# Attention half of a fused layer on eight cores: gram products reordered, three operations moved on ACT and DVE

## The chip, the cores and the metric

The kernel runs on all 8 NeuronCores of one Trainium2 chip, each with two of the sixteen sequences. A core has five engines that run their own instruction lists and meet by semaphores: TensorE (PE in the rows; its weight loads are PEld), VectorE (DVE), ScalarE (ACT), GpSimd (POOL) and SyncE (SP, here only DMA). The time is the device time in microseconds of the slowest core.

## What is computed

A pre-norm layer: x + attention(layernorm(x)), then x + ffn(layernorm(x)). The change touches the attention part only. Its core, per chunk of 64 rows and for 16 heads of 64:

```python
k = k / norm(k)
scores = q @ k.T * scale                 # 64 x 64 per head and chunk, masked
chunk_out = softmax(scores) @ v + 0.1 * (q @ M)
# then 64 sequential steps on the state M of 64 x 64:
M = M - alpha * (M k_t) k_t^T + beta * v_t k_t^T
```

The kernel does not take the 64 steps one by one. With G = k k^T (the gram matrix) the steps are a triangular system, solved by a product of six factors (I + A)(I + A^2)(I + A^4)... with A from -alpha G.

## The kernel before

phase_a (the attention half) works on NT = 32 tiles of 128 rows, a tile holding one chunk of 64 rows of each of the core's two sequences, 16 heads x 64 = 1024 columns. phase_b (the choice of experts and the two layers of the ffn) starts when phase_a has ended, and is not changed.

phase_a is one software-pipelined loop over i = -1 .. NT + 2, written out by hand for each engine, in the functions pe, act, dve, pool and sync. In iteration i the engines work on several tiles at once: i + 2 is normalised (stats, ln_steps, normal), i + 1 is transposed (x_turn), tile i is projected to k, v and q (proj), tile i - 1 = j gets its gram matrix and scores, tile i - 2 = u is solved (solve), and tile i - 3 = e ends: last factors, state update, output projection (ends). Each engine takes its instructions strictly in the order written, so an instruction that waits on a semaphore holds all that stand behind it.

PSUM: psD0 and psD1 (projections, transposes), psW (factors), and psXY, whose halves are psX (powers of A) and psY (row sums, state, outputs). gram_and_scores(j) fills both halves of psXY: 32 products, for each head h and sequence s one of a 64x64 weight (k_fm) with 128 columns (kaq_fm, holding -alpha k and q side by side). Head h writes columns hrow(h) * 128, and hrow(h) = (h % 2) * 8 + h // 2, so the even heads land in psX and the odd ones in psY. The product's place in the 128x128 array is (r, s * 64) with r = (h % 2) * 64: even heads use rows 0 to 63, odd ones rows 64 to 127, and s picks the column half.

The steps that matter, by name and line:

- TensorE, in the order of its loop: state_h(e) (L642) writes psY; state_m(e) (L653) waits for s_h; k_by_h(u) (L668) waits for s_h and s_m; q_part (L540); power_b(u, 3) (L597); factor(u, 0) (L630); row_sums(u) (L677); k_turn(i) (L551); gram_and_scores (L586), which waits for s_ka, s_qfm, s_b and s_lden; factor(u, 1); wo_part(e, 0) (L569), which waits for s_kfm; power_a(u, 4) (L597), which waits for s_g and s_exp of tile j.
- ACT: B's copy (L415), ln_steps (L405 and L407: logarithm and exponential on 128x1), rden's logarithm of the row sums in psY (L475) and its exponential (L477), then the copy of g (L483) and the exponential of the scores, PT (L484), which both read psXY.
- DVE: at an iteration's start AI[5], and the copies W, W and Wf (L829), then plus_eye 0 and 1 (AI = A + I, L825), the addition to H_sb (L868), the row sum of k's squares (L871) and its maximum with a constant (L873), plus_eye 2, the addition to M_sb (L880), xnf (L883), RHS (L886), stats (L808 to L811), plus_eye 3, W (L829), xn_tm (normal, L817), k_fm (L898), W.

Of the kernel before, what the change touches and what calls it, by code (L numbers as in the profile page):

```python
# [15 lines left out]
NH = 16  # L16
NT = 32
# [20 lines left out]
def hrow(h):  # L38
    return (h % 2) * 8 + h // 2
# [84 lines left out]
def choice_ln(s, env, n):  # L124
    rstd, s_ln = env["rstd_y"][n % 2], env["s_yln"]
    s.wait_ge(env["s_ystat"], 3 * n + 3)
    if n > 1:
        s.wait_ge(env["s_y"], n - 1)
    s.activation(rstd[:, 0:1], env["mv_y"][n % 2][:, 1:2], AF.Ln, bias=env["cst"][:, 0:1]).then_inc(s_ln, 1)  # L129
    s.wait_ge(s_ln, 2 * n + 1)  # L130
    s.activation(rstd[:, 1:2], rstd[:, 0:1], AF.Exp, scale=-0.5).then_inc(s_ln, 1)
# [9 lines left out]
def phase_a(nc, ctx, sb, ps, sem, env):  # L141
# [64 lines left out]
    s_lden = sem("s_lden")  # L206
# [8 lines left out]
    with ExitStack() as pa:  # L215
# [55 lines left out]
        def heads(ap):  # L271
            return ap.rearrange("p (h c) -> p h c", c=64)

        def by_mask(m):
            return m[:, :].unsqueeze(1).broadcast_to([128, 16, 64])
# [5 lines left out]
        def xbuf(t):  # L281

            return x_sb[(t + 3) % 7]
# [118 lines left out]
        def act(s):  # L402
            def ln_steps(t):
                s.wait_ge(s_stat, 3 * t + 3)
                s.activation(rstd[:, 0:1], mv[:, 1:2], AF.Ln, bias=cst[:, 0:1]).then_inc(s_ln, 1)  # L405
                s.wait_ge(s_ln, 2 * t + 1)
                s.activation(rstd[:, 1:2], rstd[:, 0:1], AF.Exp, scale=-0.5).then_inc(s_ln, 1)  # L407

            def power_a(u, k):
                s.wait_ge(s_pa, 5 * u + k)  # L410
                s.copy(A[k][:], psX).then_inc(s_a, 1)  # L411

            def power_b(u, k):
                s.wait_ge(s_pb, 4 * u + k)
                s.copy(B[k][:], psX).then_inc(s_b, 1)  # L415

            def k_half(i, hf):
                s.wait_ge(s_pk, 2 * i + hf + 1)
                s.copy(kraw[:, hf * 512:hf * 512 + 512], (psD0, psD1)[hf][:, :]).then_inc(s_kraw, 1)  # L419

            def v_half(i, hf):
                s.wait_ge(s_pv, 2 * i + hf + 1)
                s.copy(v_tm[i % 3][:, hf * 512:hf * 512 + 512], (psD0, psD1)[hf][:, :]).then_inc(s_v, 1)

            def q_half(i, hf):
                s.wait_ge(s_pq, 2 * i + hf + 1)
                if i > 0:
                    s.wait_ge(s_tq, i)
                s.copy(q_tm[:, hf * 512:hf * 512 + 512], (psD0, psD1)[hf][:, :]).then_inc(s_q, 1)  # L429

            s.wait_ge(s_prep, 2)
            ln_steps(0)
            def o_copy(e):
                s.wait_ge(s_po, e + 1)
                s.copy(o_fm[:, :].rearrange("p (a s c) -> p s a c", a=8, s=2),  # L435
                       psY.rearrange("p (s a c) -> p s a c", s=2, a=8)).then_inc(s_o, 1)

            for i in range(-1, NT + 3):
                u, e, j = i - 2, i - 3, i - 1
                proj = 0 <= i < NT  # L440
                solve = 0 <= u < NT
                if 0 <= e < NT:
                    o_copy(e)
                if proj:
                    k_half(i, 0)
                if solve:
                    power_a(u, 1)
                if proj:
                    k_half(i, 1)
                if solve:  # L450
                    power_b(u, 1)
                if proj:
                    v_half(i, 0)
                if solve:
                    power_a(u, 2)
                    power_b(u, 2)
                if proj:
                    s.wait_ge(s_kmax, i + 1)
                    s.activation(rk[:], kss[:], AF.Ln).then_inc(s_rk, 1)
                    s.wait_ge(s_rk, 2 * i + 1)  # L460
                    s.activation(rk[:], rk[:], AF.Exp, scale=-0.5).then_inc(s_rk, 1)  # L461
                    v_half(i, 1)
                if solve:
                    power_a(u, 3)
                if proj:
                    q_half(i, 0)
                if solve:
                    power_b(u, 3)
                if i + 2 < NT:
                    ln_steps(i + 2)  # L470
                if solve:
                    s.wait_ge(s_pden, u + 1)
                    if u > 0:
                        s.wait_ge(s_pn, u)
                    s.activation(rden[:], psY, AF.Ln).then_inc(s_lden, 1)  # L475
                    s.wait_ge(s_lden, u + 1)
                    s.activation(rden[:], rden[:], AF.Exp, scale=-1.0).then_inc(s_rec, 1)  # L477
                if i == -1:
                    s.wait_ge(s_const, NCONST)
                    s.activation(ab_sb[:, :], ab_sb[:, :], AF.Exp, scale=-1.0).then_inc(s_esig, 1)  # L480
                if 0 <= j < NT:
                    s.wait_ge(s_pg, j + 1)
                    s.copy(heads(g_sb[:, :]), gram_scores[:, :, 0, :]).then_inc(s_g, 1)  # L483
                    s.activation(heads(PT[j % 2][:, :]), gram_scores[:, :, 1, :], AF.Exp, scale=0.125).then_inc(s_exp, 1)  # L484
                if proj:
                    q_half(i, 1)
                if solve:
                    power_a(u, 4)
                    power_b(u, 4)
                if i >= NT + 1:  # L490
                    choice_ln(s, env, 2 * (i - NT - 1))
                    choice_ln(s, env, 2 * (i - NT - 1) + 1)

        def pe(t):
# [80 lines left out]
            def gram_and_scores(j):  # L575

                t.wait_ge(s_ka, j + 1)
                t.wait_ge(s_qfm, j + 1)
                if j > 0:
                    t.wait_ge(s_b, 4 * (j - 1) + 3)  # L580
                    t.wait_ge(s_lden, j)
                for h in range(NH):
                    r, hr = (h % 2) * 64, hrow(h)
                    for s in range(2):
                        c = (h // 2) * 128 + s * 64
                        ins = t.matmul(psXY[s * 64:s * 64 + 64, hr * 128:hr * 128 + 128], k_fm[j % 3][r:r + 64, c:c + 64],  # L586
                                       kaq_fm[j % 3][:, :].rearrange("p (b x) -> p b x", b=2)[r:r + 64, :, c:c + 64],
                                       start=True, stop=True, tile_position=(r, s * 64))
                ins.then_inc(s_pg, 1)
# [124 lines left out]
            for i in range(-1, NT + 3):  # L714
                u, e = i - 2, i - 3
                proj = 0 <= i < NT
                solve = 0 <= u < NT
# [84 lines left out]
        def dve(v):  # L802
# [10 lines left out]
            def normal(t):  # L813
                v.wait_ge(s_ln, 2 * t + 2)
                if t > 0:
                    v.wait_ge(s_tx, t)
                v.tensor_scalar(xn_tm[:], xbuf(t)[:], mv[:, 0:1], rstd[:, 1:2],  # L817
                                ALU.subtract, ALU.mult).then_inc(s_xn, 1)

            def plus_eye(u, k):  # L820
                if k == 0:
                    v.wait_ge(s_mask, 2 * u + 1)
                else:
                    v.wait_ge(s_a, 4 * u + k)
                v.tensor_tensor(heads(AI[k][:, :]), heads(A[k][:, :]), by_mask(eye2), ALU.add).then_inc(s_ai, 1)  # L825

            def factor(u, k):
                v.wait_ge(s_pw, 6 * u + k + 1)
                v.tensor_copy((Wf if k == 5 else W[k % 2])[:], psW[:, 0:1024]).then_inc(s_w, 1)  # L829
# [21 lines left out]
            for i in range(-1, NT + 3):  # L851
                u, e = i - 2, i - 3
                proj = 0 <= i < NT
                solve = 0 <= u < NT
# [7 lines left out]
                    factor(e, 5)  # L862
                if solve:
                    plus_eye(u, 0)
                    plus_eye(u, 1)
                if ends:
                    v.wait_ge(s_ph, e + 1)
                    v.tensor_add(H_sb[:], H_sb[:], psY).then_inc(s_h, 1)  # L868
                if proj:
                    v.wait_ge(s_sq, i + 1)  # L870
                    v.reduce_sum(kss[:, :].unsqueeze(2), heads(sq_sb[:, :]), axis=AX).then_inc(s_kss, 1)  # L871
                    v.wait_ge(s_kss, i + 1)
                    v.tensor_scalar_max(kss[:], kss[:], 1e-24).then_inc(s_kmax, 1)  # L873
# [17 lines left out]
                if solve:  # L891
                    plus_eye(u, 3)
                    factor(u, 0)
                if i + 2 < NT:
                    normal(i + 2)
                if proj:
                    v.wait_ge(s_tk, i + 1)
                    v.tensor_copy(k_fm[i % 3][:], psT).then_inc(s_kfm, 1)  # L898
                if solve:
                    factor(u, 1)  # L900
                if i == -1:
# [520 lines left out]
```

## Time and profile before

| | us |
|---|---|
| median of 3 runs | 1397.3 |
| lowest, highest | 1396.85, 1406.47 |
| the profiled execution | 1394.15 |
| its span on the slowest core (core 5) | 1392.3 |
| spans of the 8 cores | 1382.8 to 1392.3 |

Over the span TensorE is busy 83%, DVE 70%, ACT 58% and POOL 48%. The span runs from a core's first to its last instruction; the execution's time holds it and what lies around it. The loop of phase_a fills the time from about 110 to 940 us. A timeline row gives the start, the duration, the engine, the line, the operation with out<-in, the shape and the count, and in brackets the engine's idle time before it with what released it. Neighbouring instructions of one kind are merged into one row.

### The profile page before, as it was taken

To read this page: it belongs to the slowest core of one execution; us is meant where nothing else is said; L and a number is where in the kernel's file an instruction comes from. 1 tells how busy PE (TensorE), PEld (TensorE's weight loads), DVE (VectorE), ACT (ScalarE), POOL (GpSimd) and SP (SyncE) were. 2 spreads that over 40 slices of the span, in tenths; PEclk is the share of its full clock that TensorE was granted. 3 is DMA by queue.
4 is the path that set the end of the run, shared out by engine and by line. 5 is a ranking of instruction groups with operands and counts; after the bars stand their busy time and mean duration, and the time that the engine had idled before them with its cause. 6 is when DMAs were issued, how large, how long until landed. Compare 5 with 4: busy or idle time off the path is not lost. (4 is left out here: it accounts for less than half of the span.)

```text
span 1392.3 us, 68142 instructions; the slowest of 8 cores (1382.8 to 1392.3 us)
## 1 busy us (share of the span) xinstructions
PE 1148.8 (83%) x28864; PEld 692.5 (50%) x28864; DVE 980.6 (70%) x1389; ACT 810.8 (58%) x1187; POOL 672.1 (48%) x566
## 2 busy tenths in 40 slices
PE   1578988889899988889899888885677779887798
PEld 0245555555555555555555555553344556544665
DVE  3167777677777777777777777765778587785776
ACT  0155656555565555555565555654249776488775
POOL 4166766776767766777667766675101000011000
PEclk9799999999999999999999999996569799988999
DMA  9912222222222222222222222123134485750947
GB/s 160 149 44 45 43 51 51 52 48 49 47 51 55 45 49 53 47 53 43 52 50 53 50 47 40 30 34 79 23 94 143 134 263 164 217 184 35 312 135 235
DMA packets 75158, 122.09 MB, mean 88 GB/s; under 512 B 13408, under 2 KB 38000, under 8 KB 74864
## 3 DMA queue, kind: packets, MB, share of 16 engines
q1 hardware_dynamic: 48128, 92.30, 21.8%
q0 software_dynamic: 26736, 25.44, 13.6%
q8 instruction: 237, 3.88, 1.1%
q14 instruction: 57, 0.47, 0.1%
HBM read 117.93 MB, written 41.94 MB: 115 GB/s over the span
## 5 line engine op out<-in xcount | busy, mean ns | idle before, releaser
L829 DVE CAST W<-psW 128x1024 bf16<-128x1024 f32 x160 | 195.5, 1222 | 112.6 <-PE psW L630 112.4
L415 ACT CAST B<-psXY 128x1024 bf16<-128x1024 f32 x128 | 129.9, 1015 | 74.0 <-PE psXY L597 74.0
L1095 POOL TENSOR_TENSOR psel<-permT_sb,gmask_sb 128x256 bf16<-128x256 bf16 x32 | 20.1, 628 | 260.8 <-DVE permT_sb L1327 235.9
L411 ACT CAST A<-psXY 128x1024 bf16<-128x1024 f32 x128 | 129.8, 1014 | 21.2 <-PE psXY L597 21.0
L517 PE MATMUL psD<-wv_sb,xnf 128*128 128x512 bf16 x512 | 128.8, 386 | 13.6 <-DMA wv_sb<-wvT 13.6
L540 PE MATMUL psD<-wq_sb,xnf 128*128 128x512 bf16 x512 | 128.6, 385 | 11.8 <-DMA wq_sb<-wqT 6.4
L508 PE MATMUL psD<-wk_sb,xnf 128*128 128x512 bf16 x512 | 123.6, 386 | 14.6 <-DMA wk_sb<-wkT 11.8
L825 DVE TENSOR_TENSOR AI<-A,eye 128x1024 bf16<-128x1024 bf16 x160 | 131.1, 834 | 1.8 <-ACT A L411 1.3
L569 PE MATMUL psD<-wo_sb,o_fm 128*128 128x512 bf16 x512 | 131.3, 391 | 0.7 <-issue 0.6
L376 POOL TENSOR_TENSOR kt<-kraw,rk 128x1024 bf16<-128x1024 f32 x32 | 60.8, 1902 | 134.4 <-ACT rk L461 134.4
L1108 ACT CAST R<-P 128x1024 bf16<-128x1024 f32 (+1 forms) x128 | 110.1, 905 | 8.3 <-PE P L1187 6.2
L391 POOL TENSOR_TENSOR Pn<-PT,rden 128x1024 bf16<-128x1024 bf16 x32 | 68.6, 2142 | 91.1 <-ACT rden L477 91.1
L1340 DVE CAST R<-P 128x512 bf16<-128x512 f32 x128 | 81.2, 685 | 28.5 <-PE P L1214 28.2
L597 PEld LDWEIGHTS psXY<-A,B 64*64 64x64 bf16 x5120 | 57.1, 110 | 76.0 <-issue 72.9
L597 PE MATMUL psXY<-A,B 64*64 64x64 bf16 (+1 forms) x5120 | 74.9, 194 | 17.1 <-ACT PT L484 7.9
L630 PE MATMUL psW<-W,AI 64*64 64x64 bf16 x5120 | 75.7, 197 | 14.6 <-DVE W L829 7.7
L435 ACT CAST o_fm<-psXY 128x1024 bf16<-128x1024 f32 x32 | 32.4, 1012 | 94.3 <-PE psXY L684 94.3
L1144 ACT COPY ring<-P 128x1024 bf16<-128x1024 bf16 x64 | 64.6, 1012 | 37.0 <-PE P L1228 37.0
L429 ACT CAST q_tm<-psD 128x512 bf16<-128x512 f32 x64 | 37.6, 587 | 82.1 <-PE psD L540 82.1
L363 POOL TENSOR_TENSOR PT<-PT,mj 128x1024 bf16<-128x1024 bf16 x32 | 68.4, 2136 | 30.7 <-DVE AI L825 30.7
L372 POOL TENSOR_TENSOR sq_sb<-kraw 128x1024 f32<-128x1024 f32 x32 | 60.6, 1893 | 45.9 <-ACT kraw L419 28.4
L1187 PE MATMUL P<-psel,xy 64*128 64x256 bf16 x512 | 58.6, 310 | 28.5 <-ACT R L1108 22.9
(138 smaller groups left out, 2578.7 us busy)
## 6 DMA issues: line engine op xcount, KB each, us to landing
ring<-f1d SPq DMA_DIRECT2D x64, 256.0 KB, 4.0
ring<-f2d SPq DMA_DIRECT2D x64, 256.0 KB, 5.0
out<-ring SPq DMA_DIRECT2D x64, 256.0 KB, 3.4
xy<-x SPq DMA_DIRECT2D x68, 128.0 KB, 2.4
f1d<-f1w POOLq DMA_DIRECT2D x128, 64.0 KB, 2.6
f2d<-f2w POOLq DMA_DIRECT2D x128, 64.0 KB, 2.7
x1d<-x1b SPq DMA_DIRECT2D x64, 128.0 KB, 2.4
xy<-x1d SPq DMA_DIRECT2D x32, 256.0 KB, 3.5
```

Source lines behind the costliest of these rows:

```text
L411: s.copy(A[k][:], psX).then_inc(s_a, 1)
L415: s.copy(B[k][:], psX).then_inc(s_b, 1)
L508: ins = t.matmul((psD0, psD1)[hf][:, :], xn_fm[i % 2][:, kc * 128:(kc + 1) * 128], wk_sb[:, kc * 1024 + hf * 512:kc * 1024 + hf * 512 + 51 ...
L517: ins = t.matmul((psD0, psD1)[hf][:, :], xn_fm[i % 2][:, kc * 128:(kc + 1) * 128], wv_sb[:, kc * 1024 + hf * 512:kc * 1024 + hf * 512 + 51 ...
L540: ins = t.matmul((psD0, psD1)[hf][:, :], xn_fm[i % 2][:, kc * 128:(kc + 1) * 128], wq_sb[:, kc * 1024 + hf * 512:kc * 1024 + hf * 512 + 51 ...
L569: ins = t.matmul((psD0, psD1)[hf][:, :], o_fm[:, oc * 128:(oc + 1) * 128], wo_sb[:, oc * 1024 + hf * 512:oc * 1024 + hf * 512 + 512], star ...
L597: ins = t.matmul(psX[c:c + 64, hr * 64:hr * 64 + width], left[k][r:r + 64, hr * 64:hr * 64 + 64], right[k][r:r + 64, hr * 64:hr * 64 + width],
L630: ins = t.matmul(psW[c:c + 64, hr * 64:hr * 64 + 64], AI[k][r:r + 64, hr * 64:hr * 64 + 64], w_old, start=True, stop=True, tile_position=( ...
L825: v.tensor_tensor(heads(AI[k][:, :]), heads(A[k][:, :]), by_mask(eye2), ALU.add).then_inc(s_ai, 1)
L829: v.tensor_copy((Wf if k == 5 else W[k % 2])[:], psW[:, 0:1024]).then_inc(s_w, 1)
L1108: s.copy(gather_place(n, q)[:, 0:h, :, :], gathered_ps(q)[:, 0:h, :, :]).then_inc(s_ga, 1)
L1340: v.tensor_copy(place(2 * p)[:, 4 * hf:4 * hf + 4, :, :], half_tiles(P[u % 3][:, 0:512])).then_inc(s_iv, 1)
```

## The change

Four edits, all in phase_a.

1. ACT: the two operations of ln_steps(i + 2) stood ahead of rden's logarithm and now stand between rden's logarithm and its exponential.
2. TensorE: gram_and_scores takes the heads in the order of hrow (0, 2, 4, .. 14, then 1, 3, .. 15) instead of 0, 1, 2, .. 15, and waits for s_lden only ahead of the first odd head.
3. DVE: the addition to H_sb stands between plus_eye(u, 0) and plus_eye(u, 1) instead of behind both.
4. DVE: the copy of k_fm stands ahead of normal(i + 2) instead of behind it.

```diff
--- before.py
+++ after.py
@@ -466,13 +466,14 @@
                     q_half(i, 0)
                 if solve:
                     power_b(u, 3)
-                if i + 2 < NT:
-                    ln_steps(i + 2)
                 if solve:
                     s.wait_ge(s_pden, u + 1)
                     if u > 0:
                         s.wait_ge(s_pn, u)
                     s.activation(rden[:], psY, AF.Ln).then_inc(s_lden, 1)
+                if i + 2 < NT:
+                    ln_steps(i + 2)
+                if solve:
                     s.wait_ge(s_lden, u + 1)
                     s.activation(rden[:], rden[:], AF.Exp, scale=-1.0).then_inc(s_rec, 1)
                 if i == -1:
@@ -578,9 +579,10 @@
                 t.wait_ge(s_qfm, j + 1)
                 if j > 0:
                     t.wait_ge(s_b, 4 * (j - 1) + 3)
-                    t.wait_ge(s_lden, j)
-                for h in range(NH):
+                for h in sorted(range(NH), key=hrow):
                     r, hr = (h % 2) * 64, hrow(h)
+                    if hr == 8 and j > 0:
+                        t.wait_ge(s_lden, j)
                     for s in range(2):
                         c = (h // 2) * 128 + s * 64
                         ins = t.matmul(psXY[s * 64:s * 64 + 64, hr * 128:hr * 128 + 128], k_fm[j % 3][r:r + 64, c:c + 64],
@@ -862,10 +864,11 @@
                     factor(e, 5)
                 if solve:
                     plus_eye(u, 0)
-                    plus_eye(u, 1)
                 if ends:
                     v.wait_ge(s_ph, e + 1)
                     v.tensor_add(H_sb[:], H_sb[:], psY).then_inc(s_h, 1)
+                if solve:
+                    plus_eye(u, 1)
                 if proj:
                     v.wait_ge(s_sq, i + 1)
                     v.reduce_sum(kss[:, :].unsqueeze(2), heads(sq_sb[:, :]), axis=AX).then_inc(s_kss, 1)
@@ -891,11 +894,11 @@
                 if solve:
                     plus_eye(u, 3)
                     factor(u, 0)
+                if proj:
+                    v.wait_ge(s_tk, i + 1)
+                    v.tensor_copy(k_fm[i % 3][:], psT).then_inc(s_kfm, 1)
                 if i + 2 < NT:
                     normal(i + 2)
-                if proj:
-                    v.wait_ge(s_tk, i + 1)
-                    v.tensor_copy(k_fm[i % 3][:], psT).then_inc(s_kfm, 1)
                 if solve:
                     factor(u, 1)
                 if i == -1:
```

## Rows read from the trace of the kernel before

**Rows 1.** The page's first line.
```profile
span 1392.3 us, 68142 instructions; the slowest of 8 cores (1382.8 to 1392.3 us)
```

**Rows 2.** Windows: busy us (count) of PE, PEld, DVE, ACT, POOL; clock, DMA share, GB/s.
```profile
590.00:750.00 160.00, 144.42 (x4273) 83.51 (x4272) 118.44 (x145) 91.15 (x126) 111.67 (x89) 1.00 0.26 50
```

**Rows 3.** Waits, 200 to 900 us: total us, times, longest.
```profile
PE psXY L668 <- DVE M_sb L880: 18.7, 24, 1.2
PE psXY L586 <- ACT rden L475: 15.6, 23, 0.7
...
PE psXY L653 <- DVE H_sb L868: 9.3, 22, 1.2
...
PE psXY L597 <- ACT PT L484: 5.6, 23, 0.3
```

**Rows 4.** Timeline, 603 to 610 us: start us, us, engine, line; H to M.
```profile
603.01 1.73 DVE L825 TENSOR_TENSOR AI<-A,eye 128x1024 bf16<-128x1024 bf16 x2
...
603.93 0.44 PE L642 MATMUL psXY<-RHS,Wf 64*64 64x64 bf16 x32
...
604.67 1.21 DVE L868 TENSOR_TENSOR H_sb<-H_sb,psXY 128x1024 bf16<-128x1024 bf16 x1
...
605.80 1.21 DVE L871 TENSOR_REDUCE kss<-sq_sb 128x16 f32<-128x1024 f32 x1
...
607.21 0.69 DVE L825 TENSOR_TENSOR AI<-A,eye 128x1024 bf16<-128x1024 bf16 x1
...
607.82 1.21 DVE L880 TENSOR_TENSOR M_sb<-M_sb,psXY 128x1024 bf16<-128x1024 bf16 x1
...
609.18 0.44 PE L668 MATMUL psXY<-H_sb,kaq 64*64 64x64 bf16 x30 [0.93 <-DVE M_sb L880]
```

**Rows 5.** Timeline, the same place one period later.
```profile
631.90 0.45 PE L642 MATMUL psXY<-RHS,Wf 64*64 64x64 bf16 x32
...
632.72 1.21 DVE L868 TENSOR_TENSOR H_sb<-H_sb,psXY 128x1024 bf16<-128x1024 bf16 x1
```

**Rows 6.** Timeline, 612 to 619 us: ACT's chain and TensorE's steps.
```profile
612.46 1.02 ACT L415 CAST B<-psXY 128x1024 bf16<-128x1024 f32 x1
...
613.37 0.31 ACT L405 ACTIVATE rstd<-mv,cst 128x1 f32<-128x1 f32 x1
...
613.76 0.20 ACT L407 ACTIVATE rstd<-rstd 128x1 f32<-128x1 f32 x1
613.76 0.61 PE L551 MATMUL psD<-ident_bf,kt 128*128 128x128 bf16 x8
613.91 1.02 ACT L475 ACTIVATE rden<-psXY 128x1024 f32<-128x1024 f32 x1
...
615.02 1.06 ACT L477 ACTIVATE rden<-rden 128x1024 f32<-128x1024 f32 x1
...
615.08 0.64 PE L586 MATMUL psXY<-kaq,kf 64*64 64x128 bf16 x32 [0.70 <-ACT rden L475]
...
615.99 0.99 ACT L483 CAST g_sb<-psXY 128x1024 bf16<-128x1024 f32 x1
...
616.88 1.03 ACT L484 ACTIVATE PT<-psXY 128x1024 bf16<-128x1024 f32 x1
...
618.05 0.45 PE L597 MATMUL psXY<-A,B 64*64 64x64 bf16 x32 [0.21 <-ACT PT L484]
```

**Rows 7.** Timeline, 614 to 618 us: DVE.
```profile
614.83 0.81 DVE L817 TENSOR_SCALAR xn_tm<-x,mv,rstd 128x1024 bf16<-128x1024 f32 x1
...
615.54 0.69 DVE L898 COPY kf<-psD 128x1024 bf16<-128x1024 bf16 x1
...
616.14 1.22 DVE L829 CAST W<-psW 128x1024 bf16<-128x1024 f32 x1
```

**Rows 8.** Timeline, TensorE: one half of q's products.
```profile
609.93 1.90 PE L540 MATMUL psD<-wq_sb,xnf 128*128 128x512 bf16 x8
```

**Rows 9.** Timeline, TensorE, second half of the kernel: layer 1's products.
```profile
1284.93 0.77 PE L1199 MATMUL P<-R,ring 128*64 128x128 bf16 x16
```

More of the change, by code:

```diff
@@ L893, in dve @@
                     factor(u, 0)
-                if i + 2 < NT:
-                    normal(i + 2)
                 if proj:
@@ L898, in dve @@
                     v.tensor_copy(k_fm[i % 3][:], psT).then_inc(s_kfm, 1)
+                if i + 2 < NT:
+                    normal(i + 2)
                 if solve:
```

## The prediction

> **What bounds the kernel now.** I read the span and the waits of the attention half first, then the timeline of single periods. The profiled execution spans 1392.3 us on its slowest core [rows 1], and its own time is 1394.15 us, so 1.85 us lie around the span. The change touches only phase_a, so the second half is left as it is. The attention half is a loop whose period is read off two successive H additions, 604.67 and 632.72: 28.05 us [rows 4, 5]. In it TensorE is the main engine: in 160 us of the loop it is busy 144.42 us at a granted clock of 1.00, the 2.4 GHz level [rows 2], so about 2.7 us of each period are idle. The waits say where [rows 3]: in 700 us with 24 or 25 periods TensorE stood 18.7 us ahead of k_by_h for DVE's M_sb, 15.6 us ahead of the gram products for ACT's logarithm, 9.3 us ahead of state_m for H_sb and 5.6 us ahead of power_a(4) for the exponential PT. Per period that is 0.75, 0.65, 0.37 and 0.24 us, together 2.0; the other 0.7 us are pauses that no wait explains. The question is which of the four waits the change shortens, and whether another takes the time back.
>
> **Gram and scores, and the logarithm ahead of norm's operations.** Now ACT runs, from the copy of B at 612.46: norm's logarithm 613.37, norm's exponential 613.76, rden's logarithm 613.91, rden's exponential 615.02, the copy of g 615.99, PT's exponential 616.88, and TensorE's power_a(4) starts at 618.05, right after PT is done at 617.91 [rows 6]. The transposes of k are done at 614.37, so all gram products wait from about 614.3 to 615.08 for the logarithm. That wait goes: the 16 products of the even heads need only s_b, and the others find the logarithm done, because it starts at 613.37 and ends at 614.39. Its operand, the row sums, is there by then: they stand ahead of four 512-column products (0.85 us) and the transposes at 613.76, so they were issued by 612.9. So gram starts about 0.75 us sooner.
>
> That does not reach power_a(4), since this waits for the end of ACT's chain. The chain has the same six operations after B in another order. Step by step, by starts in [rows 6]: B to the next operation 0.91 (613.37 - 612.46); rden's logarithm to norm's logarithm about 0.93, its 1.02 less the overlap that B's 1.02 has with its follower; norm's logarithm to its exponential 0.39; that to the next 0.15; rden's exponential to g 0.97; g to PT 0.89; PT 1.03. Sum 5.27 us from B's start, or 617.73, against 617.91. The saving of 0.18 us is the stall between rden's logarithm and its exponential (start to start 1.11 for an operation of 1.02), which norm's operations now fill. So power_a(4) starts at 617.87: **-0.18 us a period**. g's copy waits for the last gram product, so this holds as long as gram ends ahead of 615.7.
>
> The new order costs TensorE itself something. Now consecutive products visit all four quadrants of the array and 32 of them take 0.64 us [rows 6]. Sorted by hrow, the first 16 all sit in rows 0 to 63 and alternate between two column halves, then 16 in rows 64 to 127. No row of before has this shape. From below: two at a time, 16 x 128 columns at 2.4 GHz is 0.85 us, plus the 0.2 us that one product takes beyond its columns (the 32 now are 8 x 0.053 = 0.43 of 0.64): 1.05. The nearest row is layer 1, 16 products of 128 columns alternating between column halves of the same rows in 0.77 us [rows 9]; less 0.2 that is 0.071 a pair, and 16 pairs give 1.34. From above: one at a time, 32 x 0.053 + 0.2 = 1.9 us. I take 1.05 to 1.34, nearest to the row. From 614.30 gram then ends at 615.35 to 615.64, ahead of g's copy at 615.81; TensorE is 0.3 to 0.4 us ahead of its old times until power_a(4), and waits there. With 1.9 us it would end at 616.20, g would start at 616.3 and power_a(4) at 618.36, 0.31 us later than before.
>
> In [rows 8], 8 pairs of a full weight load and a 512-column product, all on the same rows, take 1.90 us, and their 4096 columns alone are 1.71 us: the loads hide behind products in the same rows. The Trainium skill, "TensorE: Matmul & The Clock Gate", Part 3, "The mechanism", says that a weight load overlaps products in flight only where the row group differs; this speaks against the sorted order and would give the one-at-a-time price or more. By that rule the sum would be that of the serial rival below; the trace of this kernel does not agree with it.
>
> **k's copy ahead of xn.** DVE ran xn_tm at 614.83, k's copy at 615.54 and the next W at 616.14 [rows 7]. The same two operations in the other order end at the same time. k's transposes end at 614.37, in time; rstd is now ready at about 614.9, and xn_tm starts at about 615.5, in time. W is not moved. xn_tm's reader, x_turn, comes one period later. What it buys is k_fm 0.7 us sooner, which wo_part needs since TensorE now comes there sooner. Worth nothing by itself, and hidden behind the PT wait. If k's transposes were late, both would be pushed and W after them; it has about 0.9 us until its product after power_a(4) at 618.05.
>
> **H's addition between plus_eye 0 and 1.** DVE is a fixed chain here: AI0 and AI1 (1.73 us), H 604.67, the row sum of squares 605.80, AI2 607.21, M 607.82, and TensorE's k_by_h at 609.18, which stood 0.93 us for M [rows 4]. Nothing in it is idle. H waits for state_h, whose products end at 604.37; with the 0.15 us that k_by_h needs after M's end (609.03), taken as the same for every release, H could start at 604.50 instead of 604.67, 0.17 us sooner. In the next period it is 632.35 + 0.13 against 632.72, 0.24 us [rows 5]. It can't be less than nothing, and more than AI1's own time only if state_h is very early; I take 0.25. But AI1 now runs behind H and ahead of the row sum. It takes 0.61 us from start to start, as AI2 does (607.21 to 607.82). During the wait for state_h DVE is idle: behind the waiting addition stand AI1, the row sum, its maximum, AI2, M and xnf. So M, and with it k_by_h and the q products that wait for xnf, start 0.61 - 0.25 = 0.36 us later: **+0.36 us a period** (0 if H came 0.61 us sooner, 0.61 if it came no sooner). State_m gets H 0.25 us sooner, which is worth nothing, since M is behind AI2 anyway. ACT's rk logarithm and the copies queued behind it (second half of v, A3) come 0.36 us later too; A3 is read by power_b(3), which ends shortly before B's copy at 612.46 [rows 6], over 4 us behind AI2, so there is room. POOL's kt follows rk and has as much room. No transfer is moved past another; the loads of x that follow v's second half start 0.36 us later and are three periods ahead.
>
> **The sum.** The wait on M is there in each of the 29 periods with both projection and state update: 29 x 0.36 = +10.4 us. The chain to PT is shortened in some 28: 28 x 0.18 = -5.0 us. Net +5.4 us, that is 1399.5 us against the profiled 1394.15, and 1402.7 against the median of 1397.3. I say 1402.5.
>
> **The rivals.**
> - *Sorted gram runs one at a time* (slower). For it: the order leaves three of four quadrants idle if halves of the same rows can't work together. Against it: layer 1's 0.77 us for 16 [rows 9], which one at a time would be 1.05. It decides once gram takes over 1.4 us. Price at 1.9: 28 x 0.31 instead of the -5.0, with the 10.4 together +19 us: 1416. Chance 0.13.
> - *The later M is absorbed.* The 0.7 us of unexplained pauses a period may be TensorE short of instructions, and a longer stand ahead of k_by_h may be repaid by fewer pauses. Then only the -5.0 stays: 1392. For it: the pauses exist. Against: k_by_h already stands 0.75 us. Chance 0.13.
> - *The gram wait is really won* (faster). It would take a PT chain that shortens with the gram start. If all 0.65 us came through, 28 x 0.65 = 18 us less, plus 10.4: 1390; only without the H loss also would it be 1379. Against it is that power_a(4) waits for PT in 23 of 24 periods [rows 3] and that ACT has no idle time between B and PT [rows 6]. Chance 0.06.
> - My forecast: 0.60. The rest, 0.08, is for collisions that I don't see, to the slow side mostly.
>
> **How the numbers follow.** The forecast's own bounds are +0 to +0.61 for M: 29 x 0.61 - 5 = +13 above, -5 below, or 1392 to 1410. With the rivals the range is 1391 to 1415. About 1% (14 us) is what a measurement can tell from no change. Under 1383 lies only the won gram wait without the H loss and a few surprises: 0.05. Above 1411 lie the serial gram and the ill side of the rest: 0.17. Within: 0.78.
>
> **What would show it.** Right: k_by_h's wait for M_sb grows to about 1.1 us a period; the gram line waits for the logarithm no longer; power_a(4)'s wait for PT grows from 0.24 to 0.6 us; gram takes 1.05 to 1.35 us; DVE shows a new idle stretch of some 0.3 to 0.5 us between AI0 and H. Wrong: gram at 1.9 us; a wait of g's copy for TensorE; M no later after Wf than now; or the PT wait gone.

## The result

The changed kernel is slower: 1415.0 us (median of 4 runs, 1412.2 to 1417.4) against 1397.1 us for the kernel before. The ratio is 1.0119, with a 95% interval of 1.0088 to 1.0151. Measured again it was 1.0113 (1.0094 to 1.0131). The forecast was 1402.5, with a chance of 0.78 for a result within 1% (1383 to 1411); the time came out above that, at the very edge of the range of 1391 to 1415. Times here are medians of all runs; a ratio leaves out the runs in which one half of the chip ran some per cent slower, so the two can differ by a tenth of a per cent.

The span of the slowest core grew by 21.7 us (from [rows 1]); its first line now:

```profile
span 1414.0 us, 68142 instructions; the slowest of 8 cores (1395.6 to 1414.0 us)
```

The waits of the changed kernel in the same 700 us (total us, times, longest):

```profile
PE psXY L670 <- DVE M_sb L883: 25.3, 24, 1.7
...
PE psXY L599 <- ACT PT L485: 11.0, 24, 0.5
...
DVE H_sb L869 <- PE psXY L644: 6.7, 23, 0.6
```

Beside [rows 3]: TensorE's stand for M grew from 18.7 to 25.3 us (0.78 to 1.05 a period), its stand ahead of the gram products (15.6) is gone, that for PT doubled from 5.6 to 11.0, and DVE now waits for state_h. Each of these four was forecast, that for PT larger (0.6 us a period; it is 0.46). The timeline around H (start us, us, engine, line) shows how the first comes about:

```profile
612.29 1.13 DVE L827 TENSOR_TENSOR AI<-A,eye 128x1024 bf16<-128x1024 bf16 x1
...
613.21 0.44 PE L644 MATMUL psXY<-RHS,Wf 64*64 64x64 bf16 x32
...
613.79 1.22 DVE L869 TENSOR_TENSOR H_sb<-H_sb,psXY 128x1024 bf16<-128x1024 bf16 x1 [0.37 <-PE psXY L644]
...
614.93 0.68 DVE L827 TENSOR_TENSOR AI<-A,eye 128x1024 bf16<-128x1024 bf16 x1
...
615.53 1.21 DVE L874 TENSOR_REDUCE kss<-sq_sb 128x16 f32<-128x1024 f32 x1
...
616.95 0.69 DVE L827 TENSOR_TENSOR AI<-A,eye 128x1024 bf16<-128x1024 bf16 x1
...
617.56 1.21 DVE L883 TENSOR_TENSOR M_sb<-M_sb,psXY 128x1024 bf16<-128x1024 bf16 x1
...
618.92 0.47 PE L670 MATMUL psXY<-H_sb,kaq 64*64 64x64 bf16 x32 [1.53 <-DVE M_sb L883]
```

State_h's products end at 613.65 and H starts at 613.79. Before, H followed state_h's end by 0.30 and 0.37 us ([rows 4, 5]), now by 0.14. But AI1 (614.93) takes its turn behind it, and M starts 3.77 us after H instead of 3.15. The gram products and ACT's chain:

```profile
622.03 1.02 ACT L415 CAST B<-psXY 128x1024 bf16<-128x1024 f32 x1
...
623.08 1.02 ACT L473 ACTIVATE rden<-psXY 128x1024 f32<-128x1024 f32 x1
...
623.89 0.88 PE L588 MATMUL psXY<-kaq,kf 64*64 64x128 bf16 x28
624.00 0.28 ACT L405 ACTIVATE rstd<-mv,cst 128x1 f32<-128x1 f32 x1
...
624.38 0.20 ACT L407 ACTIVATE rstd<-rstd 128x1 f32<-128x1 f32 x1
624.49 1.04 ACT L478 ACTIVATE rden<-rden 128x1024 f32<-128x1024 f32 x1
...
625.43 0.99 ACT L484 CAST g_sb<-psXY 128x1024 bf16<-128x1024 f32 x1
...
626.33 1.02 ACT L485 ACTIVATE PT<-psXY 128x1024 bf16<-128x1024 f32 x1
...
627.49 0.45 PE L599 MATMUL psXY<-A,B 64*64 64x64 bf16 x32 [0.53 <-ACT PT L485]
```

From B's copy to power_a(4) it is 5.46 us, against 5.59 in [rows 6]: norm's operations fill the stall behind rden's logarithm, and TensorE waits for PT. (Neighbouring rows of gram's products are left out here: 28 of its 32 stand in the row shown, the rest mix with factor(u, 1) behind it.)

What was not forecast is in the clock. In [rows 2] the granted clock of the loop was 1.00. In the changed kernel it falls to 0.50, the 1.2 GHz level, again and again. One of these places, first in TensorE's timeline, then as windows (length, busy us and count of PE, PEld, DVE, ACT, POOL, then the clock):

```profile
206.65 0.28 PE L599 MATMUL psXY<-A,B 64*64 64x64 bf16 x9 [1.07 <-issue]
207.18 0.45 PE L670 MATMUL psXY<-H_sb,kaq 64*64 64x64 bf16 x32 [0.25 <-DVE M_sb L883]
207.78 3.17 PE L541 MATMUL psD<-wq_sb,xnf 128*128 128x512 bf16 x8 [0.16 <-DVE xnf L886]
210.87 0.64 PE L599 MATMUL psXY<-B,A 64*64 64x64 bf16 x32
```

```profile
200.00:208.20 8.20, 6.61 (x216) 3.89 (x214) 7.76 (x10) 4.60 (x8) 3.94 (x4) 1.00 0.18 42
208.20:211.60 3.40, 3.40 (x63) 1.44 (x65) 2.76 (x5) 0.51 (x1) 3.11 (x4) 0.50 0.20 25
211.60:220.00 8.40, 8.05 (x251) 5.21 (x241) 5.87 (x7) 6.94 (x11) 4.78 (x4) 1.00 0.29 59
```

The half of q's products behind k_by_h takes 3.17 us, against 1.90 in [rows 8]. TensorE had stood for 1.07 us inside power_a(3), for no wait that the profile shows, and for another 0.25 us until M was there. Over all eight cores, between 130 and 910 us, the clock was at the lower level for 14.1 us per core on average (1.3 us before), in 33 falls of 3.4 us each. They begin where k_by_h has just been let go: 32 of them start 0.5 to 1.4 us after the first product of k_by_h, thus just after TensorE's longest stand. Not every long stand brings a fall: it is 1.1 us on average in the periods with one and 1.2 us in those without.

In the kernel before, none of the falls between 130 and 910 us is at this place. It has three on all eight cores together, 16.7 to 18.0 us after the start of k_by_h, and TensorE had just stood there for 1.4 to 1.7 us in the middle of a group. Only at 923 us, near the end of the loop, do two cores show a fall behind k_by_h, after a stand of 1.37 us. One of the three, on core 1:

```profile
595.39 0.29 PE L684 MATMUL psXY<-Pn,vt 64*64 64x64 bf16 x13 [1.47 <-issue]
595.77 3.55 PE L508 MATMUL psD<-wk_sb,xnf 128*128 128x512 bf16 x8
```

For the experiments I cut the period into stretches, means in us over 208 periods of all eight cores (26 per core, from 150 us on), by the starts of the instructions named:

```
                      H to     k_by_h to  row sums   PT's end to  state_h  period
                      k_by_h   row sums   to PT end  state_h      to H
before                4.53     3.26       5.31       14.76        0.86     28.72
changed               5.14     3.48       5.09       14.84        0.61     29.16
e1 H back             4.53     3.26       5.11       14.89        0.87     28.66
e2 H alone            5.14     3.51       5.27       14.76        0.61     29.29
e4 changed, filled    5.22     3.21       5.10       14.84        0.61     28.99
e3 sort alone         4.53     3.22       5.43       14.83        0.88     28.89
e7 log and k copy     4.54     3.24       5.11       14.85        0.86     28.61
e5 eyes early         3.82     3.35       5.29       14.86        1.02     28.35
e6 e5 + gram, log     3.82     3.36       5.11       15.02        1.03     28.34
e8 e5 + log, k copy   3.80     3.34       5.11       15.03        1.03     28.31
```

### The profile page after: what moved, and what is told of

Same layout as the page of the kernel before. It is cut to its first block and busy times, and to the rows that moved or that the text cites. A ratio compares the mean times of both kernels' runs of the same rounds, so it can differ in the third digit from the quotient of the medians.

```text
span 1414.0 us, 68142 instructions; the slowest of 8 cores (1395.6 to 1414.0 us)
## 1 busy us (share of the span) xinstructions
PE 1168.4 (83%) x28864; PEld 707.5 (50%) x28864; DVE 983.3 (70%) x1389; ACT 806.5 (57%) x1187; POOL 672.8 (48%) x566
## 5 line engine op out<-in xcount | busy, mean ns | idle before, releaser
L541 PE MATMUL psD<-wq_sb,xnf 128*128 128x512 bf16 x512 | 135.5, 400 | 12.7 <-DMA wq_sb<-wqT 7.0
L827 DVE TENSOR_TENSOR AI<-A,eye 128x1024 bf16<-128x1024 bf16 x160 | 134.0, 839 | 1.9 <-ACT A L411 1.5
L632 PE MATMUL psW<-W,AI 64*64 64x64 bf16 x5120 | 80.3, 198 | 14.0 <-DVE W L831 8.1
```

What stands on the lines that cost most here:

```text
L541: ins = t.matmul((psD0, psD1)[hf][:, :], xn_fm[i % 2][:, kc * 128:(kc + 1) * 128], wq_sb[:, kc * 1024 + hf * 512:kc * 1024 + hf * 512 + 51 ...
L632: ins = t.matmul(psW[c:c + 64, hr * 64:hr * 64 + 64], AI[k][r:r + 64, hr * 64:hr * 64 + 64], w_old, start=True, stop=True, tile_position=( ...
```

## Experiments

**The changed kernel again**, on the chip of the three that follow.

> The changed kernel once more, so that the others can be compared with it on the same chip. All theories expect 1412 to 1417 us against 1395 to 1398 for the kernel before.

Measured: 1414.4 us, 1.0113 (1.0094 to 1.0131) of before.

**e1: the addition put back.** The changed kernel with this edit:

```diff
                     plus_eye(u, 0)
+                    plus_eye(u, 1)
                 if ends:
                     v.wait_ge(s_ph, e + 1)
                     v.tensor_add(H_sb[:], H_sb[:], psY).then_inc(s_h, 1)
-                if solve:
-                    plus_eye(u, 1)
```

> The changed kernel with only the addition to H_sb put back behind plus_eye 1. Theory: the addition's place costs the time (M 0.35 us later a period, some 10 us, and on top the half-clock stretches that the changed kernel shows in the loop), while the gram, logarithm and k copy edits gain 0.2 us a period. Then this gives 1390 to 1393 us, faster than before, the stand ahead of k_by_h is back at 0.75 us, and the loop has no more half-clock stretches than before. Rival: the gram, logarithm and k copy edits cause the pauses and half-clock stretches, since they pull products together and leave a longer stand ahead of power_a(4). Then this is slower than before, 1400 us or more, with half-clock stretches in the loop.

Measured: 1396.7 us, 0.9993 (0.9980 to 1.0007). The whole loss is gone, and so are the falls of the clock (0.4 us per core in the loop). The one fall left there, on core 0, does not follow k_by_h. Waits, 200 to 900 us:

```profile
PE psXY L670 <- DVE M_sb L882: 18.5, 23, 1.2
...
PE psXY L599 <- ACT PT L485: 11.5, 24, 0.5
...
PE psXY L655 <- DVE H_sb L870: 9.4, 22, 1.0
```

The stand for M is back at its 18.5 us. But the kernel is not faster than before by the 0.2 us a period that I gave the other edits: the rival (the three other edits cause the loss) is out, and the theory is half right.

**e2: the addition alone moved,** in the kernel before (the reverse of the edit above).

> The kernel before with only the addition to H_sb moved between plus_eye 0 and 1. Theory (its place costs 0.35 us a period and calls up the half clock): 1412 us or more, at most 5 us above the changed kernel, with half-clock stretches in the loop. Rival (the three other edits cause the excess over the 10 us): 1405 to 1408 us and the clock as before.

Measured: 1413.0 us, 1.0109 (1.0092 to 1.0126), the clock at its lower level for 18 us per core. So this one edit makes the loss, with and without the others. Its wait for M:

```profile
PE psXY L668 <- DVE M_sb L881: 28.1, 24, 1.7
```

**e4: the stand filled.** The changed kernel, and ahead of k_by_h four products that nothing reads:

```diff
                     power_a(u, 3)
+                    if ends:
+                        for kc in range(4):
+                            t.matmul(psW[:, 0:512], k_tm[u % 3][:, kc * 128:kc * 128 + 128],
+                                     wq_sb[:, kc * 1024:kc * 1024 + 512], start=True, stop=True)
                     k_by_h(u)
```

> The changed kernel with four 512-column products, whose result nothing reads (0.86 us a period into psW, 29 periods), put ahead of k_by_h, where TensorE stands idle for M. Nothing else differs. If the half-clock stretches come from that idle stand, they vanish from the loop and the time falls by what they cost, 5 to 8 us, to about 1408 us, although TensorE does more. If they come from elsewhere, or cost nothing that shows at the end, the time stays at 1415 or grows, by up to 29 x 0.1 us where the filling does not fit in the stand.

Measured: 1408.2 us, 1.0073 (1.0051 to 1.0094), 6.2 us less than the changed kernel on the same chip, although TensorE does more. The clock in the loop is at its lower level for 0.4 us per core, as in e1. TensorE's timeline, and its wait for M:

```profile
613.45 1.04 PE L762 MATMUL psW<-wq_sb,kt 128*128 128x512 bf16 x4
615.05 0.45 PE L670 MATMUL psXY<-H_sb,kaq 64*64 64x64 bf16 x32 [0.56 <-DVE M_sb L887]
```

```profile
PE psXY L670 <- DVE M_sb L887: 7.3, 14, 0.6
```

The stand for M shrank to 7.3 us while M itself is no sooner (H to k_by_h 5.22). So the falls come from TensorE standing idle there, and they cost about 6 us; what stays, 1.0073 or 9.6 us against the 1398.6 of before on that chip, is the later M. The table shows it as well: k_by_h to the row sums, the stretch of the q products, is 3.26 with the stand as before, 3.48 and 3.51 with the longer one, and 3.21 with the longer one filled.

The periods price a fall without any other kernel. In the changed kernel the 34 of the 208 periods that have a fall behind k_by_h last 30.05 us and the 174 others 28.98; when it ran again, 43 last 30.23 and 165 last 29.00. So a fall costs 1.1 to 1.2 us, and with 4.3 and 5.4 of them per core that is 4.5 to 6.6 us, in line with the 6.2. The periods without a fall are still 0.32 us longer than those of e1 (28.66), which is the later M by itself: 29 x 0.32 = 9.3 us.

The Trainium skill, "TensorE: Matmul & The Clock Gate", Part 1, says that TensorE's clock has two levels and falls to the lower one for want of activity. The trace agrees: 1.00 and 0.50, and filling the stand removed the falls.

**e3: the sorted order alone,** in the kernel before, with the one wait for the logarithm kept ahead of all products:

```diff
                     t.wait_ge(s_lden, j)
-                for h in range(NH):
+                for h in sorted(range(NH), key=hrow):
```

> The kernel before with only the heads of gram_and_scores sorted (even heads first); the wait for the logarithm stays ahead of all products. It measures the price of the order by itself. If halves of the same rows work together, the products take 1.05 us instead of 0.64; g's copy then waits for them some 0.1 us beyond its old start, and the rest hides behind the wait for PT: at most +0.15 us a period, 1397 to 1402 us. If they ran one at a time, 1.9 us: +0.9 us a period, over 1420 us.

Measured: 1405.1 us, 1.0047 (1.0019 to 1.0075), a little above what I had allowed. Busy time of the gram products, 200 to 900 us, before and then in e3 (line, shapes, count, busy us, mean ns):

```profile
L586 PE MATMUL psXY<-kaq,kf 64*64 64x128 bf16 x768 | 15.6, 218 | 15.6 <-ACT rden L475 15.6
```

```profile
L586 PE MATMUL psXY<-kaq,kf 64*64 64x128 bf16 x768 | 21.4, 218 | 15.3 <-ACT rden L475 15.3
```

The 24 groups take 15.6 us before and 21.4 us sorted, 0.65 and 0.89 us each. Two column halves of the same rows work together: the serial rival, 1.9 us, is out. The starts of the products in one such group show more: at its beginning and its end a pair starts every 55 ns, one product in 28 ns, but between 0.25 and 0.42 us after the first it is one in 14 ns, the pace of the old order with all four quadrants in turn. So the two row halves overlap in the middle of the group. Alone, the order costs 0.12 us in ACT's chain (row sums to PT's end 5.43), as g's copy now waits for the last product. Another 0.07 us lie behind PT and have no cause that I can show.

**e7: norm behind the logarithm and k's copy ahead of xn, alone.** The kernel before with the ACT edit and the k_fm edit of the change, gram and H as before. The kernel e1 ran once more beside it.

> The changed kernel with the H addition put back, once more beside the two below, as the measure of what the sorted order adds to them. 1395 to 1398 us.

Measured: 1396.8 us, 0.9995 (0.9979 to 1.0011).

> The kernel before with norm's operations behind the logarithm and k's copy ahead of xn, and nothing else: gram in the old order with one wait for the logarithm, the addition to H_sb in its old place. ACT's chain should be 0.18 us shorter a period, as in the kernel that has the sorted order too, which came out at 0.9993 of before. If the sorted order by itself costs what its own run says (0.5%) and this cost is there beside the other edits, the gain of ACT's chain shows here in full: -5 us, 1392. If the sorted order costs nothing once the wait is split, and the pauses eat the gain in ACT's chain, this too is within 2 us of before.

Measured: 1394.7 us, 0.9981 (0.9965 to 0.9997): by this ratio 2.7 us faster, between the two expectations. ACT's chain is shorter by 0.20 us (5.31 to 5.11; 0.18 was forecast), but the period by 0.11 only. The difference to e1, and so the price of the sorted order once its wait is split, is within the intervals.

**e5: the eyes early, a version meant to beat both.** In the kernel before, DVE's plus_eye 0 and 1 go into its idle stretches, and the row sum of squares goes ahead of H:

```diff
                     factor(e, 3)
+                    if solve:
+                        plus_eye(u, 0)
                     factor(e, 4)
+                    if solve:
+                        plus_eye(u, 1)
                     factor(e, 5)
...
-                    plus_eye(u, 0)
-                    plus_eye(u, 1)
+                    if not ends:
+                        plus_eye(u, 0)
+                        plus_eye(u, 1)
+                if proj:
+                    v.wait_ge(s_sq, i + 1)
+                    v.reduce_sum(kss[:, :].unsqueeze(2), heads(sq_sb[:, :]), axis=AX).then_inc(s_kss, 1)
                 if ends:
                     v.wait_ge(s_ph, e + 1)
                     v.tensor_add(H_sb[:], H_sb[:], psY).then_inc(s_h, 1)
                 if proj:
-                    v.wait_ge(s_sq, i + 1)
-                    v.reduce_sum(kss[:, :].unsqueeze(2), heads(sq_sb[:, :]), axis=AX).then_inc(s_kss, 1)
                     v.wait_ge(s_kss, i + 1)
```

> The kernel before with DVE's order changed so that M comes sooner: plus_eye 0 and 1 of the solve go into DVE's idle stretches ahead of the copies of factor 4 and factor 5, and the row sum of squares goes ahead of the addition to H_sb, so that the wait for state_h holds nothing up. By the timeline M then ends 0.8 to 1.0 us sooner a period. If that stand is simply taken away: 29 x 0.9, 1371 us, and no half clock in the loop. If TensorE's pauses for no wait (about 1 us a period) grow as stands are taken away, as the period of the kernel with the three other edits suggests (0.2 us won in ACT's chain, 0.06 us in the period), less than two thirds of it arrive: 1380 us or more.

Measured: 1387.0 us, 0.9923 (0.9899 to 0.9946), 10.5 us faster than before, and so some 27 us faster than the changed kernel (0.9923 against 1.0113 to 1.0119). The forecast of a stand simply taken away, 1371, is out. H to k_by_h is down by 0.71 us, and TensorE no longer waits for M in any great amount; its waits for H grew instead (9.3 us in [rows 3]):

```profile
PE psXY L653 <- DVE H_sb L876: 11.8, 22, 0.9
...
PE psXY L597 <- ACT PT L484: 5.4, 22, 0.2
```

The period fell by 0.37 us only. H itself comes 0.16 us later after state_h, since it now stands behind the row sum, and two other stretches grew by 0.1 us each: that of the q products and that from PT to state_h. The clock hardly plays a part in the former: it is at its lower level for 4 us per core in the loop, but for 0.01 us a period only in that stretch. What grew there are TensorE's pauses for no wait, from 0.06 to 0.18 us a period, while its waits for xnf and others (0.11) are gone.

**e6 and e8: e5 with the other edits of the change** (e6 with gram sorted, e8 with gram in the old order).

> The same DVE order together with the gram, logarithm and k copy edits of the change (all but the addition's place). By steps another 0.18 us a period, 5 us below the former. If the pauses take it back as they seem to, the same as the former within 2 us.

Measured: 1386.5 us, 0.9916 (0.9894 to 0.9939).

> The kernel with DVE's eyes early (1387.0 us, 0.9923 of before) and the two edits of the former, gram in its old order. If the unsorted order is worth something it is the fastest of all: 1382 us, else 1386 to 1387 like the two with eyes early.

Measured: 1387.2 us, 0.9921 (0.9904 to 0.9939). The three with eyes early are equal. ACT's chain is 0.18 us shorter in both, and the stretch from PT's end to state_h is 0.16 us longer.

## Why the prediction was right, and where it failed

The direction and the main cause were right, the size was not, and that the range holds the time is luck: the forecast's own bounds, 1392 to 1410, do not hold it. The range reached up to 1415 only for the sake of the serial gram products (1416), which did not happen.

**The later M: right in mechanism and size.** Forecast: H 0.25 us sooner, AI1 0.61 us in its place, +0.36 us a period. Measured over all cores: state_h to H 0.86 to 0.61, H to k_by_h 4.53 to 5.14, together +0.36. At the end it is worth 9 to 10 us, which e4 and the periods without a fall show with the clock's part taken out.

**The clock: the term that the sum lacked.** I took the granted 1.00 of [rows 2] as given, although the change lengthens TensorE's longest stand, and counted that stand as 0.36 us of time and nothing more. It also took the clock to its lower level for some 14 to 19 us per core in the loop, which costs 6.2 us by e4. Half of the miss of 12.5 us is this. The same stand in the kernel before is 0.3 us shorter and calls up no fall between 130 and 910 us. But behind a stand of 1.37 us at 923 us (cores 2 and 3), and behind pauses of 1.4 to 1.7 us elsewhere (cores 1 and 4), its clock did fall, so its trace held the warning that a stand of that length can cost the upper level.

**ACT's chain: right in size, but not at the end.** Forecast -0.18 us a period, measured -0.18 to -0.22, and power_a(4) does wait for PT. (The 0.93 in the forecast's chain should be 0.91, by its own reckoning; and the one period that it read, 28.05, is short of the mean, 28.72. Neither changes the sum.) The step that failed is the next: that the rest of the period keeps its length. The stretch from PT's end to state_h grew by 0.1 us in every kernel with this edit (14.76 to 14.84 and up), and by 0.16 us from e5 to e6. It grew as much in e3 (14.83) and e5 (14.86), which lack the edit, so the length alone does not show what did it. So -5.0 us came out as -2.7 with the old gram order (e7) and as -0.9, within its interval of nothing, with the sorted one (e1). This is the other part of the miss. What grows are TensorE's pauses: idle stretches for which the profile shows no releaser. On the six cores of a run whose records are complete, those of over 0.2 us add up, between 150 and 910 us, to 18.4 us per core before, 22.3 in e7, 23.4 and 24.7 in the two profiles of e1, 23.0 in e2, 18.6 in e3, 22.4 in e5, and 27 in e6 and e8. Those of over 0.15 us in the stretch from PT's end to state_h follow the ACT edit: 0.68 to 0.74 us a period in the six kernels that have it (the changed one, e1, e4, e6, e7, e8), and 0.55 to 0.62 in the four that lack it (before, e2, e3, e5). That a stand taken away comes back as pauses fits TensorE being short of instructions, but I have shown only that they grow together. Why they do stays open.

**Gram sorted: the bounds were too high.** Forecast 1.05 to 1.34 us, measured 0.89 (e3) and 0.90 (changed), since the products of the two row halves overlap where the one half follows the other, which I had not counted. It is ahead of g's copy, as forecast, so nothing hung on it here. The rule of the Trainium skill weighed in the prediction ("TensorE: Matmul & The Clock Gate", Part 3, "The mechanism"), that weight loads overlap only other row groups, would have given 1.9 us or more; e3's 0.89 us contradicts it for this shape. The serial rival gave 1416, nearly the measured time, by a mechanism that did not happen.

**k's copy: not shown.** The forecast gave it nothing by itself. It was not run alone: e7 and e1 both hold it together with ACT's edit, so their small gains can't be divided between the two.

**The sum as it should have been:** +10 for M, +6 for the clock, -1 for the other three edits: 1397 + 15 = 1412, against 1414 and 1415 in the two measurements. The 2 to 3 us left are within the intervals.

## What to carry to other kernels

An operation that waits for another engine should not be put ahead of work that is ready and that a later critical result stands behind in the same queue: its early start gained 0.25 us and the work behind it paid 0.61. Where a change lengthens the longest stand of TensorE, ask what the clock does there, even if it is at its upper level in nearly all of the trace; here four products that nobody reads, put in the stand, told it. And a stall taken out of a chain is worth only what the period shows: here between a half and nothing of it arrived.

## What the hardware showed

- The clock followed a stand of little over a microsecond. With 1.05 us of waiting for M a period on average it fell about four times per core right behind that stand in some 27 periods; with 0.78 us it did not fall there in these periods; and four filling products (1.04 us in their row) ended the falls. The five falls of the kernel before that are counted above lie behind single stands or pauses of 1.4 to 1.7 us. A fall took 3.4 us at 1.2 GHz and cost 1.1 to 1.2 us of the period.
- Products of 64x128 on one row half, alternating between the column halves, ran two at a time, and the two row halves overlapped for a while where one followed the other: 32 in 0.90 us, against 0.65 when all four quadrants are visited in turn.
- The pauses of TensorE for no wait keep to places in its list of instructions. On the six cores with complete records of the kernel before, the distance from one pause of over 0.2 us to the next (178 distances between 150 and 910 us) is always a multiple of 123 products, with as many weight loads, to within 4; often 123, 246, 492, 738 or 861. The same holds for the changed kernel (190 distances), e1, e2, e4 and e7. About half of the pauses of one core come at the same product on most others, and they take up to 1.7 us each. So they belong to the stream of instructions rather than to the work; what happens at these places no run here shows.
